# Layer norms of an eight-block kernel with a tiled spreading product and a copy on ACT, and unread products in TensorE's waits

## The reference

```python
x = x + conv_0(_ln_c(x))          # linear attention with 3x3 and 5x5 depthwise scales
t = t + ffn_0(_ln_t(t))           # 8 experts, two chosen for each token
x = x + conv_1(_ln_c(x))          # deformable convolution, gathered
t = t + ffn_1(_ln_t(t))           # FFN on the tokens that a router chooses (masked)
x = x + conv_2(_ln_c(x))          # four gates and a scan along rows
t = t + ffn_2(_ln_t(t))           # 8 experts, weighted for each position
x = x + conv_3(_ln_c(x))          # involution between two depthwise convolutions
t = t + ffn_3(_ln_t(t))           # 8 experts, one for each token, with a capacity
```

```python
def _ln(v, eps):
    m = jnp.mean(v, axis=channels, keepdims=True)
    s = jnp.var(v, axis=channels, keepdims=True)
    return (v - m) / jnp.sqrt(s + eps)
```

## Time and profile before

| what | value |
|---|---|
| median of three executions | 633.27 us (632.72 to 633.65) |
| the profiled execution, own time | 630.24 us |
| its span | 628.4 us |
| mean granted clock of TensorE in it | 0.947 |
| PE busy | 517.3 us, 82% of the span |
| DVE busy | 358.9 us, 57% |
| ACT busy | 283.9 us, 45% |
| POOL busy | 148.3 us, 24% |

### The profile page before, as it was taken

One profiled execution on the slowest core, in us unless ns is written; L12 is line 12 of the kernel. 1 busy time (PEld: TensorE's weight loads), 2 busy tenths in 40 slices (PEclk: granted clock), 3 DMA queues, 4 the chain that ended last, 5 costly groups with the idle time before them and its releaser, 6 DMA issues. The chain is left out here.

```text
span 628.4 us, 12008 instructions
## 1 busy us (share of the span) xinstructions
PE 517.3 (82%) x5122; PEld 282.6 (45%) x5122; DVE 358.9 (57%) x574; ACT 283.9 (45%) x392; POOL 148.3 (24%) x140
## 2 busy tenths in 40 slices
PE   2889989968997994777787888757997898699994
PEld 0463338834223784766766642323323234333231
DVE  1253895165556437977886456465336696722534
ACT  2452222335551218999899526443671102333330
POOL 9900000020002000897887600006003002000000
PEclk9899999998999996999999897876999999799998
DMA  7000000020000005554453000110002000000000
GB/s 272 1 3 2 2 1 2 0 96 3 0 1 30 2 6 206 197 189 158 169 197 109 2 18 1 49 39 0 0 2 108 1 0 0 2 0 1 0 18 17
DMA packets 7989, 29.90 MB, mean 48 GB/s; under 512 B 864, under 2 KB 2176, under 8 KB 7552
## 3 DMA queue, kind: packets, MB, share of 16 engines
q1 hardware_dynamic: 7936, 29.14, 13.4%
HBM read 28.47 MB, written 0.67 MB: 46 GB/s over the span
## 5 line engine op out<-in xcount | busy, mean ns | idle before, releaser
L1008 PE MATMUL PS<-GX,OH 128*128 128x64 f16 x2304 | 74.5, 196 | 25.7 <-DVE OH L1170 19.3
L1008 PEld LDWEIGHTS PS<-GX,OH 128*128 128x128 f16 x2304 | 72.0, 100 | 30.3 <-DVE OH L1170 15.3
L1095 ACT ACTIVATE DIST<-BC,wbuf 128x2048 f16<-128x2048 f16 x24 | 48.0, 2001 | 2.6 <-DMA BC<-idx_dram 0.8
L1897 DVE TENSOR_SCALAR HID<-PS,wbuf 128x512 f32<-128x512 f32 x32 | 23.8, 750 | 41.6 <-PE PS L1790 41.6
L1098 ACT ACTIVATE OH<-DIST 128x2048 f16<-128x2048 f16 x24 | 45.9, 1911 | 0.8
L1170 DVE TENSOR_SCALAR OH<-BC,wbuf 128x2048 f16<-128x2048 f16 x48 | 44.1, 942 | 2.3 <-DMA BC<-idx_dram 2.3
L943 POOL TENSOR_TENSOR V<-SQ 128x512 f32<-128x512 f32 x18 | 27.9, 1550 | 58.7 <-DVE SQ L1181 57.9
L144 PE MATMUL PS<-X,wconst 128*128 128x512 f32 x32 | 20.2, 765 | 24.0 <-DMA wconst<-pack_dram 9.7
L1786 PE MATMUL PS<-Y,wbuf 64*128 64x512 f32 x128 | 36.6, 615 | 2.3 <-DVE HID L1897 1.5
L1836 ACT ACTIVATE HID<-PS,wbuf 128x512 f32<-128x512 f32 x32 | 22.0, 687 | 36.4 <-PE PS L1790 36.4
L163 ACT ACTIVATE SQ<-PS 128x512 f32<-128x512 f32 x16 | 9.6, 597 | 63.2 <-PE PS L144 63.2
(11 more groups left out here) (301 smaller groups left out, 950.3 us busy)
## 6 DMA issues: line engine op xcount, KB each, us to landing
BC<-idx_dram SPq DMA_DIRECT2D x36, 512.0 KB, 4.0
wbuf<-pack_dram SPq DMA_DIRECT2D x1, 2082.5 KB, 11.7
wbuf<-pack_dram SPq DMA_DIRECT2D x1, 1656.0 KB, 7.0
wbuf<-pack_dram SPq DMA_DIRECT2D x1, 1494.5 KB, 6.3
wbuf<-pack_dram SPq DMA_DIRECT2D x1, 820.0 KB, 13.2
wconst<-pack_dram SPq DMA_DIRECT2D x1, 759.5 KB, 7.3
wbuf<-pack_dram SPq DMA_DIRECT2D x1, 732.0 KB, 4.1
wbuf<-pack_dram SPq DMA_DIRECT2D x1, 602.5 KB, 3.7
```

The lines of the kernel that those rows point to most:

```text
L1008: mm = pe.matmul(o, OH[:, s % NOH, qh, t * P:(t + 1) * P], src, start=(qh == 0 and part == 0), stop=(qh == 1 and part == 1))
L1095: after_act(act, act.activation(DIST[:, :], BC[:, s % NBC, :], ACT.Abs, bias=wt("negq1")))
L1897: dve.tensor_scalar(HID[:, n % 8, :], bank(2 + n % 4), wt("b1_3", 2 * e + m, 1), 0.0, ALU.add, ALU.max).then_inc(hid_in_v, 1)
```

## The change

Three things are changed.

**The spreading product.** Each of its four products takes only the 32 rows of SD and of the selecting matrix that count, as a row tile at (32q, 0), and writes a bank of its own: banks 4 to 7 for half 0, banks 0 to 3 for half 1. The multiply on DVE reads 128 columns of each of four banks. Where the target is an image, it is two instructions.

**The second copy.** The copy of half 1 is done by ACT behind its two roots (`ln_copied`); PE's spreading of half 1 and DVE's second multiply wait for it. In the blocks with an image ACT now also waits, ahead of the whole norm, until POOL has cleared the image.

**Unread products.** `keep_busy(pe, n, k)` issues k products that write bank n and that nobody reads. Four stand behind the centring, eight behind the variance of each norm; others stand in or at the end of blocks, 5 to 32 at a time.

```diff
+        def keep_busy(pe, n, k):
+            at = AT["ident"][1]
+            for _ in range(k):
+                pe.matmul(bank(n), wconst[:, at:at + 64].bitcast(BF16), wconst[:, at:at + 256].bitcast(BF16), start=True, stop=True)
...
         def ln_pe(pe, n):
             for h in range(2):
                 pe.matmul(bank(h), wt("center"), X[:, h * HC:(h + 1) * HC], start=True, stop=True).then_inc(ln_centered, 1)
+            keep_busy(pe, 4, 4)
             for h in range(2):
...
                 mm.then_inc(ln_var, 1)
+            keep_busy(pe, 4, 8)
             for h in range(2):
                 pe.wait_ge(ln_rstd, 2 * n + h + 1)
+                if h:
+                    pe.wait_ge(ln_copied, n + 1)
                 for q in range(4):
-                    mm = pe.matmul(bank(2 + h)[:, q * P:(q + 1) * P], wt("spread", q * P, P), SD[:, h * P:(h + 1) * P],
-                                   start=True, stop=True)
+                    r = 32 * q
+                    mm = pe.matmul(bank(4 * (1 - h) + q, P), wt("spread", q * P, P, r, r + 32), SD[r:r + 32, h * P:(h + 1) * P],
+                                   start=True, stop=True, tile_position=(r, 0))
                 mm.then_inc(ln_spread, 1)
...
+            o, view = out_of(1)
+            act.activation(o, view(bank(1)), ACT.Copy).then_inc(ln_copied, 1)

         def ln_dve(dve, n, out_of):
-            for h in range(2):
-                o, view = out_of(h)
-                dve.wait_ge(ln_squared, 2 * n + h + 1)
-                dve.tensor_copy(o, view(bank(h))).then_inc(ln_placed, 1)
+            o, view = out_of(0)
+            dve.wait_ge(ln_squared, 2 * n + 1)
+            dve.tensor_copy(o, view(bank(0))).then_inc(ln_placed, 1)
...
             for h in range(2):
                 o, view = out_of(h)
-                dve.wait_ge(ln_placed, 2 * n + h + 1)
+                if h:
+                    dve.wait_ge(ln_copied, n + 1)
                 dve.wait_ge(ln_spread, 2 * n + h + 1)
-                dve.tensor_tensor(o, o, view(bank(2 + h)), ALU.mult).then_inc(ln_done, 1)
+                spread = PS[:, 2048 * (1 - h):2048 * (2 - h)].rearrange("p (q c) -> p q c", q=4)[:, :, 0:P]
...
```

More of the change, by code:

```diff
@@ L101, in build @@
         stored = sem("stored")
-        ln_centered, ln_squared, ln_var, ln_sd, ln_rstd, ln_spread, ln_placed, ln_done = (sem(n) for n in (
-            "ln_centered", "ln_squared", "ln_var", "ln_sd", "ln_rstd", "ln_spread", "ln_placed", "ln_done"))
+        ln_centered, ln_squared, ln_var, ln_sd, ln_rstd, ln_spread, ln_placed, ln_copied, ln_done = (sem(n) for n in (
+            "ln_centered", "ln_squared", "ln_var", "ln_sd", "ln_rstd", "ln_spread", "ln_placed", "ln_copied", "ln_done"))
         dve_step = sem("dve_step")
@@ L178, in ln_dve, with flat_view @@
                 dve.reciprocal(SD[:, c], SD[:, c]).then_inc(ln_rstd, 1)
+            dve.wait_ge(ln_placed, n + 1)
             for h in range(2):
                 o, view = out_of(h)
-                dve.wait_ge(ln_placed, 2 * n + h + 1)
+                if h:
+                    dve.wait_ge(ln_copied, n + 1)
                 dve.wait_ge(ln_spread, 2 * n + h + 1)
-                dve.tensor_tensor(o, o, view(bank(2 + h)), ALU.mult).then_inc(ln_done, 1)
+                spread = PS[:, 2048 * (1 - h):2048 * (2 - h)].rearrange("p (q c) -> p q c", q=4)[:, :, 0:P]
+                if view is flat_view:
+                    ins = dve.tensor_tensor(o.rearrange("p (q c) -> p q c", q=4), o.rearrange("p (q c) -> p q c", q=4), spread, ALU.mult)
+                else:
+                    for b in range(2):
+                        part = o[:, b].rearrange("p (k r) w -> p k r w", k=2)
+                        ins = dve.tensor_tensor(part, part, spread[:, 2 * b:2 * b + 2].rearrange("p k (r w) -> p k r w", w=W), ALU.mult)
+                ins.then_inc(ln_done, 1)
+        def flat_view(a):
+            return a
         def flat(h):
-            return Y[:, h * HC:(h + 1) * HC], lambda a: a
+            return Y[:, h * HC:(h + 1) * HC], flat_view
         def images(a):
@@ L510, in _ @@
                 mm.then_inc(proj_ps, 1)
+                keep_busy(pe, 0, 10)
             def place(u, g):
@@ L520, in _ @@
                 act.wait_ge(w_in[0], 16)
-                ln_act(act, 0, "epsc")
+                act.wait_ge(prepared, YP_SET)
+                ln_act(act, 0, "epsc", lambda h: (images_of(YP, h), images))
                 act.wait_ge(w_in[1], 16)
@@ L1049, in _ @@
                 project(4)
+                keep_busy(pe, 4, 10)
             @block.scalar
             def _(act):
-                ln_act(act, 2, "epsc")
+                act.wait_ge(y_pad, 1)
+                ln_act(act, 2, "epsc", padded_y)
                 act.wait_ge(w_in[3], 16)
@@ L1250, in _ @@
                                   start=(m == 0), stop=(m == 1)).then_inc(hid_used, 1)
+                    if n == 0:
+                        keep_busy(pe, 4, 14)
                 pe.wait_ge(dg2_ready, 1)
@@ L1345, in _ @@
                                   start=True, stop=True).then_inc(gate_ps, 1)
+                pe.wait_ge(gate_in, 4)
+                keep_busy(pe, gbank[0], 24)
+                pe.wait_ge(gate_in, 8)
+                keep_busy(pe, gbank[0], 24)
             @block.scalar
             def _(act):
-                ln_act(act, 4, "epsc")
+                ln_act(act, 4, "epsc", flat)
                 act.wait_ge(w_in[5], 16)
@@ L1451, in _ @@
                 first(1)
+                keep_busy(pe, 5, 10)
                 for n in range(0, BEFORE_WT, 2):
@@ L1622, in _ @@
                     mm.then_inc(o_ps, 1)
+                keep_busy(pe, 0, 10)
             @block.scalar
             def _(act):
-                ln_act(act, 6, "epsc")
+                act.wait_ge(y_pad, 1)
+                ln_act(act, 6, "epsc", padded_y7)
                 act.wait_ge(w_in[7], 16)
```

18 lines of the change are left out of this document (12 added, 6 removed).

## The result

| | before | changed |
|---|---|---|
| median | 631.53 us (18 executions, 627.67 to 634.20) | 635.59 us (18 executions, 633.83 to 643.69) |
| profiled execution, own time | 630.24 us | 635.43 us |
| its span | 628.4 us | 633.6 us |
| mean granted clock | 0.947 | 0.978 |
| PE busy | 517.3 us, 82% | 557.7 us, 88% |

The ratio of changed to before is 1.0092, 95% interval [1.0063, 1.0122]: slower. It comes from the single executions; the two medians alone give 1.006.

A forecast was written before the change was run, and what follows sets the result against it. Taken as bounds: TensorE's half-clock stretches, the norm's chain and the drain at block ends. Terms +12.4 - 0.3 - 1.3 - 2.6 - 1.7 - 1.4 - 1.7 = +3.4 us on 633.27 gave 636.7 us, range 630.0 to 642.0.

The forecast's parts named there:

- The block ends: Ends of blocks: unread products outlast PE's idle room, so the next blocks start late; +12.4 us together.
- The norm: Norms at full clock: tiles and ACT's copy against twelve unread products, 0.1 us earlier each; -0.3 us over seven.
- The two norms around the gated block: Their centring products follow directly on unread products and so regain the clock: -1.7 and -1.4 us.
- The masked FFN: Fourteen unread products fit into the 3.06 us ahead of L1232 and keep PE busy: -2.6 us (0 to -3.1).
- The router of the sixth block: Low stretch from 429.1, ten products added, idle ahead of the sum not filled: -1.7 us, between +2 and -4.2.
- The first norm: Its spreading product ran at half clock, and the tiles have less to lose: -1.3 us, between 0 and -2.
- Gathering: 32 unread products, 6.9 us in 6.95 of idle before gathering; ACT sets the pace, nothing won or lost.
- A: Whole kernel: the clock gives more than the block ends cost, other low stretches go too; about 631 us, chance 0.18.
- B: Whole kernel: gain and loss cancel, within 0.2%, about 633.5 us; chance 0.15.
- C: Router, last block, norms: unread products at half clock take 0.43 us each, tiles don't overlap; 642 us, chance 0.12.
- E: Whole kernel: unread products don't lift the clock, the low stretches stay; 648 us, chance 0.03.
- D: Block ends and norms: an unread product is half as long, 0.11 us; 619 us, chance 0.04.

The follow-up runs named there:

- the fitted kernel: Changed kernel with unread products cut to fit their gaps at block ends and in the sixth block's router, three per norm: 617.91 us, ratio 0.9793 to before.

## Why the prediction was right, and where it was wrong

Direction and range held: I gave 0.63 to slower, and 635.59 us is 1.1 us under the 636.7 us forecast. It came near for the reason given, with terms that erred on both sides. In spans, the profile was to grow by 3.4 us and grew by 5.2: the block ends cost 12.8 us (forecast 12.4), and everything else gave 7.6 (forecast 9.0), of which 1.5 came from the gathering block, where nothing was forecast; and the median of before that I started from, 633.27 of three executions, is 1.7 us above that of eighteen.

**One unread product** was to be 0.37 to 0.38 us in the trace and 0.216 apart. Its mean is 0.389 us (with the few at half clock), the shortest and the median are 0.377 and 0.379, and ten take 2.32, which is 0.376 + 9 x 0.216. The step holds.

**The block ends** were to cost 12.4 us, four of them 1.43 each, the gated block 4.6. PE's idle ahead of each centring product is 0.30 us, released by PE, as said. Block two: +1.8 (forecast +1.4); block seven: +1.6 (+1.4); gated block: +3.2 (+4.6 less 1.7 for its norm, +2.9). All seven together are 12.8 us. Their net price is lower, since they also carry the clock: without them the kernel is 6.6 to 8 us faster. With the ends fitted and the norm with them it is 18 us less than the changed kernel.

**The norm** was to gain 0.1 us; it gained 0.00, and the tiles were read 0.64 us after their start, where I had 0.65. The reciprocals start 3.64 us after the first centring product, 0.4 us later than before, where I had 0.2. In the two blocks with a padded image the norm is 0.13 us longer, inside the 0 to 0.2 of the two multiplies, and the wait for the cleared image is hidden as said; without products behind the centring it shows (n = 6 takes 6.4 us in the fitted kernel, n = 2 takes 6.1). ACT has this wait in the first norm too, which the prediction left out; nothing is waited for there. The step that the twelve products eat what tiles and copy give is right (6.03 us without them).

**The two norms around the gated block** were to regain 1.7 and 1.4 us. They took 8.75 and 8.48 us and now take 7.08 each. Both centring products run at full clock; the timeline shows one against the 3.63 us of the earlier trace rows:

```profile
395.13 3.63 PE L146 MATMUL PS<-wconst 128*128 128x512 bf16 x16
399.06 1.96 PE L150 MATMUL PS<-X,wconst 128*128 128x512 f32 x4 [0.30 <-PEq L1225]
```

**The masked FFN** is the first term that failed: "Fourteen products (3.0 us) fit into the 3.06 us ahead of L1232" was to give 2.6 us, and the block grew by 0.1 where 1.2 less was forecast, its end included. The aimed stretch did go. Behind an earlier one the clock is 1.00 to the end of the block, and from the `up` products behind the filling to DVE's last instruction it is 9.6 us instead of 12.6 (3.1 was the most). But the earlier stretch, which the prediction had left out of its terms, became twice as long: 3.4 us before, from about 374.5 to 377.9, and 6.8 us now. What stands ahead of those `up` products takes 1.6 us more. The rows by stretch, before and then twice changed, and the changed kernel's timeline with sixteen router products of two columns and then five products that take 4.09 us:

```profile
374.50:377.90 3.40, 3.36 (x6) 1.24 (x5) 2.36 (x4) 1.88 (x5) 0.00 (x0) 0.50 0.00 0
```

```profile
373.50:380.30 6.80, 6.80 (x18) 3.59 (x18) 2.93 (x7) 2.30 (x7) 0.00 (x0) 0.51 0.00 0
380.50:399.00 18.50, 18.26 (x71) 6.32 (x69) 13.66 (x44) 12.60 (x38) 0.00 (x0) 1.00 0.00 0
```

```profile
372.61 2.55 PE L1254 MATMUL PS<-wbuf,Y 128*128 128x2 f32 x16 [0.67 <-DVE Y L197]
375.09 2.08 PE L1260 MATMUL PS<-Y,wbuf 64*128 64x512 f32 x4
377.10 4.09 PE L1269 MATMUL PS<-DIAG,wconst 128*128 128x512 f32 x5
```

In every profile on record, the kernel before included, a low stretch begins at this place, 6 to 11 us behind the block's start, 3.4 or 6.8 us long, so it isn't an accident of one execution; that the narrow products are its cause was not tried alone.

**The router of the sixth block** failed likewise: -1.7 us forecast, about 0.2 measured (the block's -0.2 is its end's +1.4, its norm's -1.4, and the rest). "Its idle ahead of the sum is not filled" was seen and not taken far enough. PE idles 3.2 us there (2.9 before), the stretch at half clock still begins 0.9 us before it ends and is 6.8 us long instead of 10.2, and the ten products behind it then ran at half clock themselves, 3.80 us instead of 2.32:

```profile
432.61 0.99 PE L1456 MATMUL PS<-wbuf,SUM 128*128 128x8 f32 x4 [3.19 <-DVE SUM L1569]
433.53 2.08 PE L1463 MATMUL PS<-Y,wbuf 64*128 64x512 f32 x4
435.55 3.80 PE L146 MATMUL PS<-wconst 128*128 128x512 bf16 x10
```

With three products in place of these ten, and the other fitted ones, the block is 5.0 us shorter than before; with eight more in the idle time it runs at 1.00 and is 5.8 us shorter.

**The first norm** was to gain 1.3 us and lost 0.3 (10.64 to 10.91 us): the unread products stand in its chain too, the first four of them at half speed (1.91 us). The block is 0.6 us shorter all the same, as forecast in sum, since two stretches of 3.4 us at half clock, from 16.1 and from 46.8, are gone. The mechanism there was wrong, the number right by luck: in the second profile of the changed kernel the norm takes 9.82 us, both stretches are there again (from 20.0 and from 47.4), and the block is 1.6 us longer than before.

**Gathering** was to give nothing inside the block and pay 1.4 us at its end. It stayed at 168.8 us, so 1.5 us were won inside. The 32 unread products are not what won it: the first sample is gathered 0.62 us later in the block than before, the second 0.10 us later. The 1.5 us come at one place, between the fifteenth and the sixteenth of the 36 samples, and stay the same from there on. In the kernel before and in the changed one, PE's gathering products around it:

```profile
286.33 2.20 PE L1008 MATMUL PS<-GX,OH 128*128 128x64 f16 x70 [0.96 <-issue]
290.38 2.04 PE L1008 MATMUL PS<-GX,OH 128*128 128x64 f16 x64 [1.85 <-DVE OH L1170]
```

```profile
287.24 2.03 PE L1033 MATMUL PS<-GX,OH 128*128 128x64 f16 x64 [0.83 <-DVE OH L1198]
289.60 1.57 PE L1033 MATMUL PS<-GX,OH 128*128 128x64 f16 x48 [0.33 <-DVE OH L1198]
```

Before, PE sat idle for 0.96 us in the middle of a sample with nothing that the profile shows to wait for, and then waited 1.85 us for DVE's comparison for the sixteenth sample, where the changed kernel waits 0.33. This is in one execution of each kernel, and I have no cause for it.

**The rivals.** A, that the clock gives more than the ends cost, has its first half: half clock fell by 39 us. But that is worth at most 19 us where PE is the bound, and what stood against it was the 12.4 of the ends plus the twelve products of each norm. B did not come: the interval begins at 1.0063. The 624 us that the prediction gives for A's side prices no work that outlasts its gap, and that work was 12.8 us. C was seen in part, in the router's ten products (3.80 us) and the first norm's four (1.91), not in the tiles. E is dead: products do lift the clock. D too.

## What to carry to other kernels

Unread products that keep the array busy are worth something (1.9% here with the old norm, 2.6% together with the new one), if each group is over before the wait that it stands in ends: work out the gap from the timeline, divide by the length of one, and round down, above all at a block end, where the drain waits for the last of them. An edit that takes work from TensorE and shortens its chain can bring it more time at half clock and so lose its gain again: judge such an edit with the gaps already filled, by its time and not by the length of the stage. Filling gaps isn't enough for that: behind the tiles and a router the clock fell with no idle time over 0.33 us. The new norm gave nothing alone; with the gaps filled it gave 0.9 to 1.6 us of 7.3 in one pair of kernels and 4.5 to 6.5 in another, in both with overlapping intervals, and of its two parts the tiles, which shorten the norm most, don't show in the time. Put the filling where PE idles ahead of the stretch that fell to half clock, and not inside it.

## What the runs showed of the hardware

- A norm that was 1.05 us shorter, with no other edit, did not make the kernel faster; it has 80 to 104 us at half clock in twelve executions, against 55 to 79 in 23 of the kernel before. I had not expected an edit of the norm to move TensorE's clock by that much. With filled gaps the half clock goes with the row tiles (26 to 51 us, against 18 to 24 with full spreading products), not with ACT's copy.
- In the first norm the four passes of centring took 3.75 us (3.43 before), about as long as four passes take at half clock elsewhere (3.63). The traces hold no record of the clock there: the first record, at full clock, begins 3.0 us after the first product in the kernel before and 6.1 us after it in the changed one, and a table by stretch prints 1.00 for the time ahead of it. So the speed at the start of a launch is to be read from the products' lengths.
- Row tiles of 32 by 128 stood between full-width products in every norm. They were read 0.64 to 0.67 us after their start, against 1.26 for the full ones, and eight passes are 0.50 us. The Trainium skill, "TensorEngine Tiling (Array Packing)", section "Key Properties", says that a change of tiling mode drains TensorE; no cost of that can be seen in the norm's length, which the tiles shortened by 0.7 us; that they shortened the kernel's time isn't shown.
- Executions of one program differ in their time at half clock, and their time goes with it: from 23 to 42 us of half clock at 633.8 to 637.3 us to 45 to 51 us at 640.2 to 643.7. In the profile of one of the latter there are more, short stretches at half clock, spread over six of the eight blocks. What decides how many there are stays open.
